# The masked decay exponent of a chunked scan moved from GpSimd to VectorE, and TensorE's order of work inside a step

## The reference, cut to what matters

```python
la = jnp.log(a).reshape(nb, nc, Q)
cs = jnp.cumsum(la, axis=-1)
L = jnp.where(tri, jnp.exp(cs[..., :, None] - cs[..., None, :]), 0.0)
scores = jnp.einsum('znid,znjd->znij', Cc, Bc) * L
y_diag = jnp.einsum('znij,znjh->znih', scores, Xc)
...
out = y * jax.nn.silu(res)
return out @ w_out.T
```

## Time and profile before

| | |
|---|---|
| median of 3 executions | 2626.51 us (2623.35 to 2630.94) |
| the profiled execution | 2623.35 us, with a span of 2621.8 us from first to last instruction |
| mean granted TensorE clock | 0.948 |
| TensorE matmul, share of the span | 90% |
| VectorE | 57% |
| GpSimd | 42% |
| ScalarE | 37% |

### The profile page before, as it was taken

How to read it: one execution, slowest core, us unless ns; L and a number is a source line. 1 busy time by engine, 2 the same in 40 slices (tenths; PEclk the granted TensorE clock), 3 DMA queues, 4 the chain that set the end, 5 groups by cost and what they waited for, 6 DMA issues and landing times. The chain is left out here.

```text
span 2621.8 us, 48248 instructions
## 1 busy us (share of the span) xinstructions
PE 2361.0 (90%) x12839; PEld 1796.3 (69%) x12840; DVE 1496.3 (57%) x3155; ACT 981.7 (37%) x2202; POOL 1091.1 (42%) x990
## 2 busy tenths in 40 slices
PE   7969999996756899999999949999989998899998
PEld 5855545553535888888888827888866665788886
DVE  6435666662665445555555554999536665655554
ACT  3114545553253344444444432222245554311111
POOL 3128888883004566666666411111146664000000
PEclk9978999998867999999999969999999999999999
DMA  5459999994355899999999653446679770100001
GB/s 180 128 171 330 340 340 336 354 329 176 121 212 132 233 275 270 252 248 264 266 244 232 99 161 110 168 168 192 193 197 214 176 185 12 38 25 24 24 9 65
DMA packets 263308, 491.20 MB, mean 187 GB/s; under 512 B 31889, under 2 KB 149137, under 8 KB 253458
## 3 DMA queue, kind: packets, MB, share of 16 engines
q1 hardware_dynamic: 197202, 272.17, 34.3%
q0 software_dynamic: 62976, 212.42, 28.8%
q10 hardware_dynamic: 3024, 5.29, 0.6%
HBM read 592.96 MB, written 198.79 MB: 302 GB/s over the span
## 5 line engine op out<-in xcount | busy, mean ns | idle before, releaser
L1421 PE MATMUL m_ps_u<-m_ring,m_xT_hi 128*128 x1280 | 373.5, 353 | 23.2 <-DMA m_ring<-w_split 18.3
L1387 POOL DMA_INDIRECT expert_sum<-x_res,token_of x160 | 253.1, 1582 | 223.3 <-ACT x_res L1489 121.3
L798 ACT ACTIVATE probs<-ps_c 128x512 f32<-128x512 f32 (+3 forms) x384 | 182.8, 490 | 210.8 <-PE ps_c L731 136.3
L1421 PEld LDWEIGHTS m_ps_u<-m_ring,m_xT_hi 128*128 128x128 f32 x1280 | 238.9, 191 | 27.8 <-issue 27.5
L828 DVE TENSOR_REDUCE neg_max<-ps_r 128x1 f32<-128x512 f32 (+3 forms) x256 | 147.6, 590 | 153.8 <-PE ps_r L698 102.5
L1421 PE MATMUL m_ps_u<-m_ring,m_xT_lo 128*128 x640 | 218.4, 341 | 0.0
L1380 POOL DMA_INDIRECT m_xg<-x_rows,token_of x160 | 175.7, 1098 | 100.6 <-issue 94.5
L1544 DVE SCALAR_TENSOR_TENSOR m_h<-m_silu,m_xg,m_ps_u 128x128 f32<-128x128 f32 x160 | 55.7, 348 | 269.1 <-ACT m_silu L1483 229.6
L698 PE MATMUL ps_r<-k_st,q_st 96*128 96x512 f32 (+3 forms) x384 | 162.0, 429 | 46.6 <-DVEq L821 19.6
L1858 PE MATMUL s_ps<-s_x_hi,s_w_hi 128*128 128x512 f32 x512 | 199.7, 390 | 1.5 <-POOL s_w_lo L1828 1.5
L1858 PE MATMUL s_ps<-s_x_lo,s_w_hi 128*128 128x512 f32 x512 | 199.2, 389 | 0.0
(11 more groups left out here) (354 smaller groups left out, 5759.7 us busy)
## 6 DMA issues: line engine op xcount, KB each, us to landing
m_ring<-w_split SPq DMA_DIRECT2D x160, 1536.0 KB
m_ring<-w_split SPq DMA_DIRECT2D x160, 768.0 KB
w_split<-e_gu_parts POOLq DMA_DIRECT2D x32, 1536.0 KB
proj<-s_out SPq DMA_DIRECT2D x32, 1024.0 KB, 3.9
e_raw_gu<-w_experts POOLq DMA_DIRECT2D x32, 768.0 KB, 9.0
w_split<-e_dn_parts POOLq DMA_DIRECT2D x32, 768.0 KB
e_raw_dn<-w_experts POOLq DMA_DIRECT2D x32, 512.0 KB
q_st<-q_parts SPq DMA_DIRECT2D x32, 256.0 KB
```

What stands on the lines that cost most here:

```text
L798: nc.scalar.activation(probs[a][j % RING][:, :width], ps_c[a][:, :width], ACT.Exp, scale=SCALE).then_inc(exp_done, 1)
L1387: pool.indirect_dma_start(acc[j % 2], rows_at(j), y[j % TURNS], None, bounds_check=PADDED - 1, oob_is_err=True, compute_op=ALU.add).then_i ...
L1421: last = nc.tensor.matmul(ps_u[b % 2][:, :W_UP], x[b % 2][:, k, :], ring[:, first + k * GU_ROW:][:, bass.ds(place, W_UP)], start=(n == 0), ...
```

## The change

GpSimd keeps only the copy to `bx_now`. The exponent moves to a new function `weigh` on VectorE, which does difference and mask in one instruction for each of the four sequences, 128x128 each, with the scalar taken from a column of `csT` whose address lies in a register. It stands at the head of VectorE's step n, for step n + 1, and before the loop for step 0. The waits for `cs_loaded` and `y_done` move with it; the semaphore between the two old instructions goes. On TensorE the order of a step becomes for all k: `prepare` of n + 1, `new_states` of n, projection, `outputs` of n.

```diff
             with pool.Fori(0, BODIES) as it:
                 for b in range(2):
                     for k in range(STEPS):
-                        n = (it * 2 + b) * STEPS + k
                         if k == 0:
                             pool.wait_ge(bx_loaded[b], it * 64 + 64)
                             pool.sem_inc(turns_begun, 1)
-                        pool.wait_ge(sc_done, n + 1)
+                        pool.wait_ge(sc_done, (it * 2 + b) * STEPS + k + 1)
                         pool.sem_inc(turns_begun, 1)
                         nc.gpsimd.tensor_copy(bx_now[k % 2][:, :, :].rearrange("p s (h t) -> p s h t", t=CHUNK_TOK),
                                               bx[b][:, :, :].rearrange("p h (s k t) -> p s k h t", s=SEQS, t=CHUNK_TOK)[:, :, k, :, :]).then_inc(bx_ready, 1)
-                        if k == 0:
-                            pool.wait_ge(cs_loaded[b], it * 16 + 16)
-                            pool.sem_inc(turns_begun, 1)
-                        pool.wait_ge(y_done, n + 1)
-                        pool.sem_inc(turns_begun, 1)
-                        cs_chunk = cs_all[b][:, :].rearrange("p (s k i) -> p s k i", s=SEQS, i=P)[:, :, k, :]
-                        own = csT[:, bass.ds((it * 2 + b) * NC, NC)].rearrange("p (s k) -> p s k", s=SEQS)[:, :, k:k + 1]
-                        nc.gpsimd.tensor_tensor(att[k % 2][:, :, :], cs_chunk, own.to_broadcast([P, SEQS, P]), ALU.subtract).then_inc(differences, 1)
-                        pool.wait_ge(differences, n + 1)
-                        pool.sem_inc(turns_begun, 1)
-                        nc.gpsimd.tensor_tensor(att[k % 2][:, :, :], att[k % 2][:, :, :], mask[:, :].rearrange("p (o i) -> p o i", o=1).to_broadcast([P, SEQS, P]),
-                                                ALU.add).then_inc(expo_done, 1)
...
                 for b in range(2):
                     for k in range(STEPS):
-                        if k > 0 and not (first and b == 0):
-                            project_out(*last_group(it, b), k)
                         if not (final and b == 1 and k == STEPS - 1):
                             prepare(*after(it, b, k))
-                        if k == 0 and not (first and b == 0):
-                            if first:
-                                pe.wait_ge(w_loaded, 16)
-                            project_out(*last_group(it, b), k)
                         if k < LINKS:
                             new_states(it, b, k)
+                        if first and b == 1 and k == 0:
+                            pe.wait_ge(w_loaded, 16)
+                        if not (first and b == 0):
+                            project_out(*last_group(it, b), k)
                         outputs(it, b, k)
...
+            def weigh(it, b, k):
+                g = it * 2 + b
+                n = g * STEPS + k
+                if k == 0:
+                    dve.wait_ge(cs_loaded[b], it * 16 + 16)
+                dve.wait_ge(y_done, n + 1)
+                for s in range(SEQS):
+                    c = s * STEPS + k
+                    last = nc.vector.scalar_tensor_tensor(att[k % 2][:, s, :], cs_all[b][:, c * P:(c + 1) * P], csT[:, bass.ds(g * NC + c, 1)],
+                                                          mask[:, :], ALU.subtract, ALU.add)
+                last.then_inc(expo_done, 1)
...
                         more = not (final and b == 1 and k == STEPS - 1)
+                        if more:
+                            weigh(*after(it, b, k))
                         if 0 < k < LINKS:
                             decay_state(it, b, k)
...
+            weigh(0, 0, 0)
             apply_decay(0, 0, 0)
```

More of the change, by code:

```diff
@@ L2090, in scan @@
             sem(n) for n in ("x_out", "b_out", "att_done", "st_done", "dec_done", "state_done", "y_mm_done", "gated_done", "o_done", "o_added_s")]
-        differences = sem("s_differences")
         block = ctx.enter_context(nc.Block())
```

## The result

The changed kernel takes 2651.2 us (median of 7) against 2630.9 for the kernel before in as many runs: ratio 1.0079, 95% interval 1.0054 to 1.0102, so slower by some 21 us. The forecast was no measurable change, 2627.4 within 2619 to 2643. It was wrong.

The account below looks back on a forecast made before the run. TensorE's own work was taken to set the step in the groups that project. Terms 4.8 - 0.9 - 5.5 + 1.4 + 1.7 - 0.6 = +0.9 us gave 2627.4 us against a median of 2626.51, range 2619 to 2643.

Parts of the forecast that it names:

- What bounds the kernel: In the scan's groups that project, TensorE's own work sets the 4.40 us step; removing GpSimd's instructions gives 0.
- The chain on VectorE: VectorE's step after the change: gatings 1.22, new block 0.81, ScalarE's exponential 1.12, decay product 0.60; sum 3.75 us.
- contention: VectorE's new block is held up by GpSimd's copy: 0.3 us a step, 0.5 where TensorE sets the step.
- The scaled state's stall: VectorE's scaled state, 0.96 us long beside GpSimd's mask add, would last near 0.3 after the change.
- One sign that the prediction had called wrong: GpSimd's copy inside VectorE's new block, with one member near 0.7 us long, would show the forecast wrong.
- First group: Scan's first group, without projection: steps go from 3.36 to 4.05 us, +4.8; the wait for w_out goes, -0.9.
- Waits at the borders and at the end: TensorE's waits at six borders between projecting groups go, -5.5 us; the last step's wait for the gatings goes, -0.6.
- New stalls of VectorE in the groups that project: VectorE needs 4.85 us in steps with an output add; slack absorbs all but 0.1: 14 x 0.1 = +1.4 us.
- TensorE's own work is the same instructions in another order: In projecting steps, only transposes behind outputs lengthen, 0.66 for 0.60: +3.4 us if real, 0 if modelled; +1.7 taken.
- VectorE becomes the bound everywhere: Rival: each GpSimd copy is waited for in full, a step costs 4.43 us; +15.9, 2642 us, chance 0.22.
- half rate: Rival: VectorE's new instruction runs at half rate, 4.58 us a step; +25.3, 2652 us, chance 0.04.
- The granted clock: Rival: TensorE's clock falls to its lower level, 0.50, in the first group; +8, 2635 us, chance 0.06.

Follow-up runs that it names:

- the padded loop: The kernel before, with eight increments of an unused semaphore added to each of the sixteen steps in VectorE's loop body; ratio 1.0048 to the kernel before.
- the written-out loop: The changed kernel with VectorE's loop over groups 2 to 5 written out, so its queue never branches back; ratio 1.0048 to the kernel before.

## Why the prediction was wrong, point by point

**What bounds the kernel** held: TensorE set the steps that project, and GpSimd's work was not in their way.

**The chain on VectorE** held. 3.75 us and 0.3 of contention made 4.05 a step, measured 4.05. The four new instructions take 1.28 from the first start to the next line's, where 4 x 0.27 was 1.08; the excess of 0.20 is the contention, in place of 0.3 (the other 0.1 lies between scaled and new state, 0.41 in place of 0.31). The scaled state's stall went as forecast. One sign that the prediction had called wrong did come, though: GpSimd's copy runs inside the new block and stretches one member, here the first, and the second in the groups that project:

```profile
1945.40 0.62 POOL L2154 COPY bx_now<-early 128x512 f32<-128x512 f32 x1 [3.43 <-PE s_ps_sc L2178]
1945.59 0.57 DVE L2309 SCALAR_TENSOR_TENSOR s_att<-early,csT,scan_mask 128x128 f32<-128x128 f32 x1
2052.65 0.70 DVE L2309 SCALAR_TENSOR_TENSOR s_att<-cs_all,csT,scan_mask 128x128 f32<-128x128 f32 x1
```

The copy was under way when the first of these members began, and the member ends 0.14 us behind it. So here the side that began later waited, which the prediction had left open. The block takes 1.28 us in the first group, 1.41 in most steps of the others and 1.06 behind the pause, where no copy runs: the copy costs VectorE 0.2 and 0.35 us, where 0.3 and 0.5 were reckoned, and the projecting steps had room for it.

**First group**: forecast 4.8 - 0.9 = +3.9, measured 36.76 - 32.89 = +3.9. That it is exact is luck in part. From the first transposes to the fifth both kernels take 13.6 us; the 0.69 a step holds for the next five, +3.45 in place of +4.8, and the rest up to the first projection gives +0.4 in place of -0.9, since the last scores wait 1.10 us for VectorE and the state products now stand ahead of that projection.

**Waits at the borders and at the end**: forecast -5.5 and -0.6; the changed kernel's waits show them gone.

**New stalls of VectorE in the groups that project** (+1.4): none but the pause, as the order had room for VectorE's work; in the old order it costs the 3.3 us at the borders.

**The step that failed first: "TensorE's own work is the same instructions in another order".** I had seen the transposes at 0.66 rather than 0.60 behind the outputs, and took half of its +3.4. Measured: the rest of the scan is 8.6 us longer by the order alone, although the border waits are gone too, where the forecast for order, borders and last step together was -5.5 + 1.7 - 0.6 = -4.4: 0.30 us for each of 42 full steps is 12.6, and the borders give back some 4 net. The row pointed the right way; the term was taken from one pair of neighbours where four distances grew (by 0.06, 0.10, 0.09 and 0.05). The trace of before had three of the four at hand, since around its borders the pieces stood in another order: transposes of 0.66, outputs followed after 0.58 or 0.59 where scores stand ahead of them, and state products behind the projection of 2069.46, 1.91 us after it:

```profile
2071.37 0.45 PE L2205 MATMUL s_ps_st<-x_nat,b_dec 128*64 128x64 f32 x8
```

The trace agrees with a sentence of the Trainium skill (TensorEngine Tiling (Array Packing), section Key Properties), by which changing the tiling mode, not just the tile, drains TensorE, in so far as the steps grow with the number of such changes; a drain itself is no row of it. I had not weighed it; it speaks against this order.

**The step that was missing: a row for VectorE's queue itself.** The change adds 128 instructions to the loop's body (64 of them address computations, which the after trace lists), and the pause where the loop turns back costs 9.1 us. The sum had no term for it, so it stood at nothing; I had costed only their time on the engine. The Trainium skill (Runtime: NRT & Kernel Launch, section Instruction fetch mechanics) says that a taken branch whose target is no longer in the window held must fetch it first; the padded loop, the written-out loop and the packets of the instruction queue agree.

**The rivals.** Measured is about +20 us. "VectorE becomes the bound everywhere" gave +15.9 and half rate +25.3, both near it by mechanisms that did not happen: in the groups that project the scores wait for VectorE in one place, behind the pause, not in most steps. Half rate is out: a new instruction has a median of 346 ns with both inputs in SBUF, and the pair with one in PSUM has 0.34 and 0.35. The granted clock fell only behind the pause; in the first group it is 0.50 at the start, as before, and 1.00 from 1941 us on.

The sum of what was measured: first group +3.9, order +8.6, pause +9.1, together 21.6, the scan's whole difference. It holds along one path: first the loop is written out (9.1), then the exponent goes back to GpSimd (3.9 in the first group, nothing in the rest), then the old order comes back (8.6). With the exponent left on VectorE, the old order gives back only 5.3 (252.98 less 247.70), the borders keeping 3.3; and in the old order the pause costs 6.0.

What stays open: whether it is the array's shape as such that keeps the weights from being loaded ahead, or the part of the array in which the tiles lie; every order tried changes both together. Why the padded loop pauses twice and the changed kernel once, and from which length on a loop pauses, was not tried: bodies of about 226 instructions in the trace had none, bodies of about 355 had one or two.

## What to carry to other kernels

Before moving a block of matmuls, write down for each neighbour how it uses the array (rows x columns of its weights), count the places where that changes, and price the new ones by a start-to-start distance in the trace; a TensorE that is "busy" and waits for nobody can still lose 7% of a step to its own order. When work moves to an engine that runs a loop, count the instructions that its body gains, address computations too. And where a dependence is late once per group, shifting the dependent work by one step in every step, in an order that keeps good neighbours, beats a special order for that step.

## What the runs showed of the hardware that was not expected

- Same matmuls, no wait: 4.70 us a step with six changes of shape between neighbours, 4.35 to 4.40 with four. Behind the projection (128x128), the transposes' first weights (128x128) are loaded 0.43 us ahead; those of a 128x64 or 64x128 piece are not, and the loader idles for 0.76.
- VectorE stood for 5.0 to 6.8 us where its loop turned back, once the body had grown by some 128 instructions, and 6 more packets went through an instruction queue. TensorE, idle for 6.6 us of the changed kernel's pause, then had a granted clock of 0.50, and the loss was 9.1 us; with the old order TensorE idled for 4.0 and the loss was 6.0.
- A GpSimd copy of 0.62 to 0.69 us beside four VectorE instructions with two SBUF inputs costs VectorE 0.2 us when the copy began ahead of the four, 0.35 when it began during the first or the second.
